# Cross attention: the last two rounding steps of a finished unit's outputs on VectorE, directly behind its copy, in place of GpSimd

## What is computed

```python
kvx = jnp.einsum('bsi,oi->bso', cond, w_kv_x)
kx, vx = jnp.split(kvx, 2, axis=-1)
kx = _ln(kx.reshape(b, sc, g, d), kxln_w, kxln_b)
xout = _gqa(qx, kx, vx).reshape(b, s, nh * d)
cat = jnp.concatenate([core, xout], axis=-1)
catq = _div_clamp_fp8(cat, proj_smooth)      # divide, clip at 448, to bf16, round to fp8 (e4m3)
return jnp.einsum('bsi,oi->bso', catq, wproj) * (proj_in_scale * proj_w_scale)
```

## Time and profile before

| | us |
|---|---|
| median of 3 runs | 2467.07 (2463.65 to 2467.97) |
| the profiled execution | 2462.99 |
| its span, first to last instruction | 2461.1 |
| PE busy | 2305.7 (94%) |
| PE weight loads busy | 2019.9 (82%) |
| DVE busy | 2005.9 (82%) |
| ACT busy | 1066.8 (43%) |
| POOL busy | 944.7 (38%) |

### The profile page before, as it was taken

The page is one execution under the profiler, slowest core; times in us unless marked ns, Lnnn a source line. Parts: engine busy times, 40 slices in busy tenths (PEclk is TensorE's granted clock), DMA queues, the critical chain, the costliest instruction groups (busy, mean ns, idle before and its releaser), DMA issues. The chain is left out here.

```text
span 2461.1 us, 37753 instructions
## 1 busy us (share of the span) xinstructions
PE 2305.7 (94%) x12485; PEld 2019.9 (82%) x12485; DVE 2005.9 (82%) x3874; ACT 1066.8 (43%) x1826; POOL 944.7 (38%) x640
## 2 busy tenths in 40 slices
PE   7999999999995788867999999999999999998998
PEld 5777777879993566646999999999999999997898
DVE  8999988877766878865888988888889888887347
ACT  1000101018872666642555555555555555555233
POOL 5555200200003244441455555554555555556000
PEclk9999999999997888878999999999999999999999
DMA  9677543347643111124122222212222222114511
GB/s 386 257 281 301 218 151 122 145 150 251 225 156 123 57 61 46 44 71 162 50 91 79 84 79 87 74 51 86 90 77 86 79 86 73 52 63 148 204 53 53
DMA packets 171773, 304.51 MB, mean 124 GB/s; under 512 B 58769, under 2 KB 140770, under 8 KB 166562
## 3 DMA queue, kind: packets, MB, share of 16 engines
q1 hardware_dynamic: 165650, 283.18, 33.3%
q0 software_dynamic: 6032, 20.20, 2.2%
HBM read 214.35 MB, written 89.00 MB: 123 GB/s over the span
## 5 line engine op out<-in xcount | busy, mean ns | idle before, releaser
L1971 PE MATMUL ps<-s_qc,s_ct 128*125 128x448 f32 x2304 | 522.5, 376 | 1.3 <-issue 1.3
L1999 PE MATMUL ps<-s_p_hi,s_cn 125*128 125x448 f32 x1536 | 472.5, 369 | 2.8 <-DVE s_p_lo L2094 2.3
L1971 PEld LDWEIGHTS ps<-s_qc,s_ct 128*125 128x125 f32 x2304 | 420.2, 187 | 50.4 <-issue 12.9
L1852 POOL TENSOR_TENSOR keep_x<-keep_x,s_sx 125x896 f32<-125x896 f32 x128 | 288.9, 2257 | 233.3 <-DVE s_mxh L2115 113.8
L577 DVE BATCH_NORM_STATS2 s_st<-ps 125x6 f32<-125x128 f32 x1472 | 304.8, 281 | 46.2 <-PE ps L447 39.1
L1916 ACT ACTIVATE s_sx<-s_sx 125x896 f32<-125x896 f32 x192 | 182.2, 949 | 350.6 <-DVE s_sx L2088 350.6
L1999 PEld LDWEIGHTS ps<-s_p_hi,s_cn 125*128 125x128 f32 x1536 | 289.6, 189 | 29.0 <-DVE s_p_lo L2094 5.0
L2075 DVE TENSOR_TENSOR s_sx<-ps,keep_krs 125x896 f32<-125x896 f32 x192 | 208.8, 1088 | 122.0 <-PE ps L1971 118.3
L1999 PE MATMUL ps<-s_p_lo,s_cn 125*128 125x448 f32 x768 | 281.5, 367 | 0.0
L2094 DVE TENSOR_TENSOR s_p_lo<-s_sx,s_p_hi 125x896 fp32r<-125x896 f32 x192 | 258.8, 1348 | 2.7 <-ACT s_p_hi L1921 2.7
L2115 DVE TENSOR_TENSOR s_mxh<-s_mxh,s_sx 125x896 f32<-125x896 f32 x128 | 217.3, 1697 | 0.1
(11 more groups left out here) (393 smaller groups left out, 4823.7 us busy)
## 6 DMA issues: line engine op xcount, KB each, us to landing
l_ahead<-in_ctxt SPq DMA_DIRECT2D x16, 1500.0 KB, 8.0
s_ct<-ct_hi SPq DMA_DIRECT2D x48, 500.0 KB, 4.4
s_ct<-ct_lo SPq DMA_DIRECT2D x48, 500.0 KB, 5.1
s_cn_raw<-in_ctx SPq DMA_DIRECT2D x48, 500.0 KB
l_raw<-in_ctxt SPq DMA_DIRECT2D x15, 1500.0 KB, 10.4
l_raw<-in_w SPq DMA_DIRECT2D x16, 1024.0 KB, 5.1
ct_hi<-l_hi SPq DMA_DIRECT2D x8, 1500.0 KB, 12.6
ct_lo<-l_lo SPq DMA_DIRECT2D x8, 1500.0 KB, 16.1
```

What stands on the lines that cost most here:

```text
L1852: pool.tensor_tensor(a, a, p[:, PR * w.pt:PR * w.pt + PR, :], ALU.add).then_inc(s["acc_ready"], 1)
L1971: mm = pe.matmul(sc[st % 2][:, j, :], a[:, k, at:at + TT], x[w.h][:, k, :], start=(c == 0), stop=(c == 5))
L1999: mm = pe.matmul(pv[:, k, :], x[:, t, k * P:k * P + P], y[w.vr][:, j, :], start=(t == 0 and c == 0), stop=(t == NT - 1 and c == 2))
```

## The change

The add and the subtract leave POOL's list, where they stood at the end of step 3, and stand in DVE's list in step 3, directly behind the instruction that makes c, with the same semaphores. The wait for the store of the unit before (`cat_stored`) goes with them. Nothing else is changed; the lines below shift by 8 up to there and by 1 behind.

```diff
--- before.py
+++ after.py
@@ -1858,14 +1858,6 @@
                         pool.wait_ge(s["cn_hi_ready"], NCH * b + c + 1)
                         at = slice(CHT * c, CHT * c + CHT)
                         pool.tensor_tensor(cn_lo[:, at, :], cn_raw[c][:, :, :], cn_hi[:, at, :].bitcast(F32), ALU.subtract).then_inc(s["cn_lo_ready"], 1)
-                    if w.i == 3 and w.three_back:
-                        d = w.u - 3
-                        pool.wait_ge(s["cc_ready"], d + 1)
-                        pool.tensor_tensor(cs[:, :], cb[:, :], cc[:, :], ALU.add).then_inc(s["cs_ready"], 1)
-                        if not (static(d) and d < 1):
-                            pool.wait_ge(s["cat_stored"], 16 * d)
-                        pool.wait_ge(s["cs_ready"], d + 1)
-                        pool.tensor_tensor(cat[:, :], cs[:, :], cc[:, :], ALU.subtract).then_inc(s["cat_ready"], 1)
                 steps_of(pool, None, run)
 
             @block.scalar
@@ -2105,6 +2097,13 @@
                         dve.tensor_scalar(ce[:, :].bitcast(U16), cb[:, :].bitcast(U16), 0x7F80, None, ALU.bitwise_and).then_inc(s["ce_ready"], 1)
                         dve.wait_ge(s["ce_ready"], w.u - 2)
                         dve.tensor_scalar(cc[:, :], ce[:, :], 2.0 ** -6, 1.5 * 2.0 ** 20, ALU.max, ALU.mult).then_inc(s["cc_ready"], 1)
+                        d = w.u - 3
+                        dve.wait_ge(s["cc_ready"], d + 1)
+                        dve.tensor_tensor(cs[:, :], cb[:, :], cc[:, :], ALU.add).then_inc(s["cs_ready"], 1)
+                        if not (static(d) and d < 1):
+                            dve.wait_ge(s["cat_stored"], 16 * d)
+                        dve.wait_ge(s["cs_ready"], d + 1)
+                        dve.tensor_tensor(cat[:, :], cs[:, :], cc[:, :], ALU.subtract).then_inc(s["cat_ready"], 1)
                     if w.new and w.i >= 1:
                         dve.wait_ge(s["sc_read"], w.n + 1)
                         a = sx[w.h][:, 0:PR, :] if w.i == 1 else mxh[:, :, :]
```

## The result

The changed kernel takes 2490.6 us (median of 4 runs, 2488.36 to 2493.55) against 2466.61 (4 runs) before: ratio 1.0102, 95% interval 1.0089 to 1.0115, **1.0% slower**. The prediction said 2493.

A forecast was written before the change was run, and what follows sets the result against it. The prediction took TensorE's matmul list, busy 969.92 of 970 us, as the bound. Both terms, 1.88 us a pair over 14 pairs, made 26.3 us: 2467.07 + 26 = 2493 us, range 2472 to 2500.

The forecast's parts named there:

- x: DVE's lateness behind step 3 from the two added instructions: 1.32 us, bounds 0.63 and 2.2.
- First term: At the broadcast L2016 in odd units, PE waits for the late reciprocal through ACT: 0.68 us a pair.
- room: Time from ACT's end to PE's arrival at broadcast L2016: 0.68 us in odd units, 1.37 in even.
- Second term: At step 0 of even units POOL's L1860 takes the port before DVE's L2094, delaying PE's transposes: 1.20 us a pair.
- Sum: 14 pairs × 1.88 = 26.3 us over the median 2467.07, giving 2493 us, 1.05% slower.
- that tail: In the last two units DVE sets the pace; x is added, port time given back: booked 0 (±1) us.
- rival 3: PE's clock falls after the new wait at L1979, 22 us if in every pair: 2515 us; chance 0.05.
- Rival 1: L2094 keeps the port at step 0; PE loses 5 to 9.5 us in all: 2474 us; chance 0.15.
- Rival 2: Hidden: x within the room of 0.68, L2094 first at step 0, no PE waits: 2463 to 2467; chance 0.14.

The follow-up runs named there:

- run 7: Run 1's kernel with VectorE's two new instructions run a second time, into tiles nobody reads; 2482.43 us, ratio 1.0073.
- run 2: The changed kernel with GpSimd's third context chunk made to wait for VectorE's low-part subtraction of step 0; 2471.88 us, ratio 1.0036.
- run 1: The changed kernel with VectorE's step-3 reciprocal moved ahead of the rounding; 2462.43 us, ratio 0.9999.
- run 3: The changed kernel with the subtraction back on GpSimd at its old place, the sum staying on VectorE; 2460.05 us, ratio 0.9993.
- run 8: The kernel before with only VectorE's reciprocal moved behind the scaling of step 4's scores; 2477.78 us, ratio 1.0056.
- run 6: The changed kernel with GpSimd still running two same-size instructions at the old place, on tiles nobody reads; 2489.06 us, ratio 1.0101.

## Why the prediction was right

- **x, DVE's lateness behind step 3: 1.32 predicted, 1.40 measured.** The durations were right (626 ns both). The missing 0.08 is mostly the gap ahead of the second instruction, 0.10 in place of 0.03 (1734.67 to 1734.77). That instruction waits for two semaphores, the sum's and the store's; in run 7 the second copy of it, with no wait for a store, follows the second copy of the sum by 0.03 (1730.14 to 1730.17).
- **First term: 0.68 a pair predicted, 0.94 measured (run 2 against run 1).** The prediction's own rule holds: PE is late by what the reciprocal is late, less the room, plus the 0.04 to 0.05 from ACT's end to PE's start. Both latenesses, against the kernel before, counted from the last L1985 ahead, means of 13 units:

| | room | reciprocal late | PE's broadcast late |
|---|---|---|---|
| the change, odd units | 0.68 | 1.39 | 0.76 |
| the change, even units | 1.37 | 1.39 | 0.08 |
| run 3, odd units | 0.68 | 0.65 | 0.02 |
| run 8, odd units | 0.68 | 1.09 | 0.46 |
| run 8, even units | 1.37 | 1.77 | 0.46 |

So with x = 1.40 the odd unit's term is 0.76 instead of 0.68, and even units, booked at nothing since 1.32 fits into 1.37, are touched too. PE's wait in the profile, 0.6, is smaller than its lateness because it is counted from the end of the matmul ahead, and PE's matmuls overlap: in the kernel before the broadcast starts 0.16 ahead of that end. What the prediction left out comes behind the start: where the broadcast waits for ACT, its two matmuls start 0.48 apart in place of 0.38, and only part of that is made good later. Odd units grow by 0.79 in all (35.90 in run 2, 35.11 in run 1), even ones by 0.15 (35.25 and 35.10).
- **Second term: the port changes hands at step 0, 1.20 predicted, 1.15 measured.** The change is 1.30 a pair longer than run 2, but 0.15 of that the kernel before loses at the product as well (70.36, against 70.21 in run 1, where PE waits nowhere). POOL was expected 0.2 ahead and is 0.36 ahead. L2086 was expected to take 3.1 and takes 3.02; it ends at 1753.30, 0.96 behind POOL (1752.34). The rule of the Trainium skill (SBUF — State Buffer, Who interferes with whom), that the port pair is locked for a whole instruction, is what this row shows.
- **Sum: 14 × 1.88 = 26.3 predicted for the pairs; 29.06 measured from the 3rd to the 30th L1985.** Against it stand the last units and what follows, booked at 0 ± 1 and measured at −3.64. The two errors nearly cancel: 25.4 between the two profiles, 24.0 between the medians. The mechanism was right, but that the total came within 2.4 us is in part luck.
- **The term that failed is that tail.** "x is added there and the port time given back" did happen: the last unit's step-5 maximum takes 1.08 in place of 3.03, and its fold ends 0.45 earlier than before, counted from the 31st L1985. The other 1.5 of that unit goes with the clock, which the prediction looked for as a loss (rival 3) and not as a gain. PE's timeline there, of before, of after and of run 2:

```profile
2229.26 0.81 PE L1979 MATMUL ps<-keep_ident,s_mx 125*112 125x125 f32 x4 [4.66 <-DVE s_ca L2098]
2229.73 0.72 PE L1999 MATMUL ps<-s_p_hi,s_cn 125*128 125x448 f32 x1
...
2233.71 0.36 PE L1985 MATMUL ps<-s_diag,s_ones_r 112*125 112x448 f32 x1
```

```profile
2257.86 0.61 PE L1971 MATMUL ps<-keep_ident,s_mx 125*112 125x125 f32 x4 [2.74 <-DVE s_ca L2090]
2258.22 0.45 PE L1991 MATMUL ps<-s_p_hi,s_cn 125*128 125x448 f32 x1
...
2260.75 0.36 PE L1977 MATMUL ps<-s_diag,s_ones_r 112*125 112x448 f32 x1
```

```profile
2240.05 0.94 PE L1973 MATMUL ps<-keep_ident,s_mx 125*112 125x125 f32 x4 [2.74 <-DVE s_ca L2092]
...
2244.53 0.37 PE L1979 MATMUL ps<-s_diag,s_ones_r 112*125 112x448 f32 x1
```

From the transposes to L1985 it took 4.45, and now takes 2.89. The windows view shows the clock (columns as in the earlier trace rows): before, the stretch from the transposes on and one some 30 us behind the last L1985; after, the same two; and run 2, the first of them:

```profile
2229.60:2232.90 3.30, 3.30 (x12) 2.95 (x11) 2.79 (x3) 2.07 (x5) 3.29 (x2) 0.50 1.00 426
...
2263.70:2267.00 3.30, 3.30 (x10) 2.48 (x11) 1.22 (x1) 2.29 (x9) 0.00 (x0) 0.50 0.94 357
```

```profile
2257.80:2261.10 3.30, 3.25 (x17) 2.74 (x17) 2.60 (x3) 1.88 (x5) 3.30 (x2) 1.00 0.00 0
...
2290.80:2294.10 3.30, 2.10 (x13) 1.73 (x14) 1.10 (x1) 3.14 (x11) 0.00 (x0) 1.00 1.06 381
```

```profile
2240.10:2243.40 3.30, 3.30 (x11) 3.01 (x12) 2.37 (x3) 1.65 (x5) 3.30 (x2) 0.51 0.00 0
```

PE stood 4.66 ahead of the transposes before and 2.74 in the change, but the length of this wait alone does not decide the clock: run 2 has the same 2.74 and runs at the lower level (1.2 GHz), with 4.48 from the transposes to L1985. So the 1.5 is shown to go with the clock; why the clock stayed up in the change is not shown, and this part of the gain can't be put down to the edit.

- **Rivals.** Rival 1 (the low part keeps the port) is what run 2 makes of the change: ratio 1.0036, which on 2467 is 2476, where it said 2474. Rival 2 (hidden) is what run 3 shows for one instruction instead of two. (The 1.39 to 1.45 us that it sets against 626 ns are means of rows from 1.03 to 1.91 us, since GpSimd waits for the port as well; the shortest is 1.6 times 626 ns.) Rival 3 (the clock falls in the steady part) did not come: 1.00 throughout, although PE stands for 1.1 and 0.6 in every pair.

## What to carry to other kernels

Before giving an engine that others wait for more work, list what stands behind the new place in its queue, and for each the room until its reader wants it: the price is the lateness beyond that room, not the engine's idle share. A tiny instruction with a reader on the bound engine (here a reciprocal of 4 columns) belongs ahead of long ones that nobody waits for; moved there, the same change costs nothing here. Where two engines share a port, a late start of some tenths can hand it to the other side, so compare start times at the next race and not only durations.

## What the runs showed of the hardware

- An add with bf16 inputs and an f32 output takes DVE 626 ns for 448 elements, the same as with f32 inputs.
- Between VectorE and GpSimd a start earlier by 0.05 to 0.07 was enough to have the port: POOL 0.05 ahead, DVE's low part took 3.03 (run 6); DVE 0.07 ahead, it took 1.08 and POOL's chunk 3.27 (run 1), in place of 2.40 (run 2).
- PE's idle time in the profile can be smaller than its lateness: 0.6 shown where the broadcast came 0.76 late, since in the kernel before it starts 0.16 ahead of the end of the matmul ahead of it.
- In the last unit the granted clock behind PE's idle time ahead of the transposes was 0.50, the 1.2 GHz level, after 4.66 (before), 2.74 (run 2) and 2.75 (run 7), and 1.00 after 2.74 (the change) and 2.77 (run 3). The length of that idle time does not tell the two apart; what does stays open.
- The part behind the last L1985, where all kernels have the same matmuls, took from 225.74 (the change) to 231.61 us (run 6). Stretches at 0.50 lie at different places in them. I have not tried how much of the difference these explain, so a difference of up to 5 us between whole programs is here not to be read as the edit's. The pairs of units within a run agree to about 0.1 us, so the edit is read from them.
